# Preparing output weights behind the first exponentials, and placing one weight matrix with GpSimd

## What is computed

```python
q = rope(norm(x) @ Wq.T); k = rope(norm(x) @ Wk.T)          # bf16
o = where(causal, exp(q @ k.T / 128**0.5), 0).sum(-1)       # one number per row
a = relu(o @ fc1_w.T + fc1_b) @ fc2_w.T + fc2_b             # 1 -> 16 -> 128
x = x + norm(a)
h = relu(norm(x) @ W1[1] + b1[1])                           # the gate always picks expert 1
y = h @ W2[1] + b2[1]
x = x + norm(y)
```

## Time and profile before

| | |
|---|---|
| median of 3 runs | 93.13 us (92.77 to 93.2) |
| profiled execution | 92.96 us, its span 91.2 us |
| TensorE busy | 82.5 us, 90% of the span |
| VectorE busy | 78.5 us, 86% |
| ScalarE busy | 70.7 us, 78% |
| GpSimd busy | 59.2 us, 65% |
| granted TensorE clock | 0.992 of full speed |

### The profile page before, as it was taken

The page is one execution under the profiler, slowest core; times in us unless marked ns, Lnnn a source line. Parts: engine busy times, 40 slices in busy tenths (PEclk is TensorE's granted clock), DMA queues, the critical chain, the costliest instruction groups (busy, mean ns, idle before and its releaser), DMA issues.

```text
span 91.2 us, 1530 instructions
## 1 busy us (share of the span) xinstructions
PE 82.5 (90%) x445; PEld 49.4 (54%) x445; DVE 78.5 (86%) x205; ACT 70.7 (78%) x201; POOL 59.2 (65%) x84
## 2 busy tenths in 40 slices
PE   4958999988899789998999999999999999999930
PEld 1327465544354145433553368684575985599920
DVE  4469998999998999999998988998799689894961
ACT  5035899996998899999999999988669629545750
POOL 6497887808700697976914058587799944995590
PEclk9999999999999999999999999999999999999996
DMA  1989988830505050005000000000403101205283
GB/s 39 268 252 298 285 267 227 208 88 0 115 7 115 7 115 4 0 0 115 0 0 0 7 0 0 0 0 0 115 0 90 36 4 53 62 0 163 67 235 110
DMA packets 11884, 7.64 MB, mean 84 GB/s; under 512 B 851, under 2 KB 10980, under 8 KB 11876
## 3 DMA queue, kind: packets, MB, share of 16 engines
q1 hardware_dynamic: 11876, 7.55, 30.6%
HBM read 3.61 MB, written 2.10 MB: 63 GB/s over the span
## 4 chain that ended last, share of the span: by engine, by line
PE 59%; ACT 14%; DVE 9%; DMA 7%; issue 3%; SPq 2%; POOL 2%; POOLq 1%; DVEq 0%
PE psum L724 19%; PE psum L798 14%; ACT psum L553 11%; PE psum L750 11%; PE psum L716 6%; DMA x_s<-x 4%; PE psum L777 3%; DMA qk_swap<-qk 3%; DVE rows_n L348 2%; POOL rstd L489 2%; ACT fc L566 2%; DVE qk_r L383 2%; DVE qk_swap L383 2%; PE psum L769 1%; DVE qk L505 1%
## 5 line engine op out<-in xcount | busy, mean ns | idle before, releaser
L489 POOL TENSOR_TENSOR rstd<-ve,half_neg 128x4 f32<-128x4 f32 (+2 forms) x38 | 35.0, 930 | 23.1 <-DVE ve L354 18.7
L553 ACT ACTIVATE psum<-psum 128x1024 f32<-128x1024 f32 (+7 forms) x48 | 36.6, 763 | 1.2 <-PE psum L754 0.8
L750 PE MATMUL psum<-qk_r 128*128 128x512 bf16 (+3 forms) x80 | 19.7, 348 | 1.7 <-DVE qk_r L417 1.0
L798 PE MATMUL psum<-w_c,hid 128*128 128x128 f32 x128 | 16.0, 277 | 0.0
L798 PEld LDWEIGHTS psum<-w_c,hid 128*128 128x128 f32 x128 | 15.5, 192 | 0.8 <-issue 0.3
L724 PE MATMUL psum<-cols_n,wqk 128*128 128x512 f32 (+1 forms) x36 | 15.8, 553 | 0.0
L724 PE MATMUL psum<-cols_n,w_c 128*128 128x512 f32 (+1 forms) x36 | 15.7, 550 | 0.0
L750 PEld LDWEIGHTS psum<-qk_r 128*128 128x128 bf16 x80 | 6.7, 98 | 13.0 <-ACT psum L553 4.8
L716 PE MATMUL psum<-ident,rows_n 128*128 128x128 f32 x64 | 10.2, 277 | 0.9 <-DVE rows_n L348 0.9
L638 DVE BATCH_NORM_STATS2 stats<-psum 128x6 f32<-128x256 f32 x23 | 8.7, 419 | 1.5 <-PE psum L798 1.0
L664 DVE SCALAR_TENSOR_TENSOR x<-psum,rstd,x_s 128x128 f32<-128x128 f32 x32 | 9.1, 343 | 1.0 <-POOL rstd L489 0.9
(11 more groups left out here) (84 smaller groups left out, 129.8 us busy)
## 6 DMA issues: line engine op xcount, KB each, us to landing
x_s<-x SPq DMA_DIRECT2D x7, 256.0 KB, 4.3
qk_swap<-qk SPq DMA_DIRECT2D x14, 128.0 KB, 2.3
out<-x_s SPq DMA_DIRECT2D x7, 256.0 KB, 2.4
table<-tables SPq DMA_DIRECT2D x3, 256.0 KB, 4.2
x_s<-x SPq DMA_DIRECT2D x2, 128.0 KB, 3.6
table<-tables SPq DMA_DIRECT2D x2, 128.0 KB, 3.8
w_f<-w SPq DMA_DIRECT2D x2, 128.0 KB, 3.2
out<-x_s SPq DMA_DIRECT2D x4, 64.0 KB, 1.7
```

Source lines behind the costliest of these rows:

```text
L489: ready[k].done(eng.tensor_tensor(rstd[:, g, STAT_SLOT[k], t], ve[:, g, STAT_SLOT[k], t], half_neg[:, 0:tiles], ALU.pow), n)
L553: exps.done(eng.activation(area, area, ACT.Exp, scale=scale_qk, accum_out=sums[:, g, s, j:j + 1]), n, j, s)
L750: mm = eng.matmul(psum[:, own[0] + i, 0:width], query, qk_r[:, g0 + c, 1, 0:width], start=True, stop=c < gb)
L798: mm = eng.matmul(bank[:, j * P:(j + 1) * P], hid[:, g, h, (j0 + j) * P:(j0 + j + 1) * P], w2_c[:, h, :], start=not seeded and h == 0, sto ...
```

## The change

Four things are edited.

1. `+fc` becomes one activation over 128x128 that writes the centred, repeated matrix into a new tile `fc2_c`.
2. A new step `fcspread` on GpSimd makes fc2 from it, with two selects over 128x512: the first copies `fc2_c` to each of the four column blocks and zeroes partitions below 32j, the second, in place, zeroes those from 32(j+1) on. `fc2` matmuls wait for it. VectorE's clearing of fc2 is gone. `+hT` waits for `fcmean` instead of `+fc`.
3. `w2mean` and `w2`, which stood apart in the front, stand together behind `exp.2.0.0`.
4. `b2mean`, which stood in the front, stands behind `exp.3.3.0`.

The order is otherwise the same, word for word.

```diff
@@ STEPS @@ (the lines wrap anew; only these words move)
-... load_table.4 k.6#4 cos.3.D w2mean.0 load_b1.0 eps1.2.D q.6#0 ... swap.4 cos.4.D w2.0 q.0#3 ...
-... k.0#2 b2mean.0 rope.3.D swap.6 ...
+... load_table.4 k.6#4 cos.3.D load_b1.0 eps1.2.D q.6#0 ... swap.4 cos.4.D q.0#3 ...
+... k.0#2 rope.3.D swap.6 ...
+... norm1.5.P scores.3.0.0#12 exp.2.0.0 w2mean.0 w2.0 +k.8.D scores.3.1.0#67 exp.3.0.0 fcspread.0 rstd1.7 rot.1#5
+sum.2.D scores.3.3.0#34 swap.8 cos.8.D exp.3.1.0 hT.2#0 rot.0#1 sin.1.D cos.0.P k.2#2 exp.3.3.0 b2mean.0 sin.0.D
@@ gpsimd @@
+            def spread_fc():
+                taken["fc"].wait(eng, 0)
+                eng.affine_select(out=fc2[:, :, :], in_=fc2_c[:, :].unsqueeze(1).to_broadcast([P, TILES, P]),
+                                  compare_op=ALU.is_ge, fill=0.0, base=0, pattern=[[-BLOCK, TILES], [0, P]],
+                                  channel_multiplier=1).then_inc(s_fc, 1)
+                eng.wait_ge(s_fc, 1)
+                fc_spread.done(eng.affine_select(out=fc2[:, :, :], in_=fc2[:, :, :], compare_op=ALU.is_ge, fill=0.0,
+                                                 base=BLOCK - 1, pattern=[[BLOCK, TILES], [0, P]],
+                                                 channel_multiplier=-1), 0)
@@ take, hT @@
-                    taken["fc"].wait(eng, 0)
+                    mean_fc.wait(eng, 0)
@@ scalar, +fc @@
-                    eng.wait_ge(s_zero_fc, 1)
-                    for j in range(TILES):
-                        r = slice(BLOCK * j, BLOCK * (j + 1))
-                        ins = eng.activation(fc2[r, j, :], bank_of("fc", 0)[r, P:2 * P], ACT.Identity,
-                                             bias=means[r, 2:3])
-                    taken["fc"].done(ins, 0)
+                    taken["fc"].done(eng.activation(fc2_c[:, :], bank_of("fc", 0)[:, P:2 * P], ACT.Identity,
+                                                    bias=means[:, 2:3]), 0)
@@ vector @@
-            eng.memset(fc2[:, :, :], 0.0).then_inc(s_zero_fc, 1)
@@ tensor, fc2 @@
                     taken["hT"].wait(eng, n)
+                    fc_spread.wait(eng, 0)
```

More of the change, by code:

```diff
@@ L43 @@
 stat1.5 load_w2.0 +fc.0 rstd1.0 norm1.6.D q.3#1 load_table.2 eps1.8.D norm1.0.D tr1.6#4 +k.3.D rstd1.8 +q.3.A k.4#0
[L44 to L77, removed]
+eps1.5.D +tr1.1.A stat1.2 swap.3 +tr1.6.A norm1.8.P tr1.0#3 stat1.7 +k.4.A q.1#1 load_table.4 k.6#4 cos.3.D load_b1.0
@@ new lines @@
+eps1.2.D q.6#0 +tr1.0.D rstd1.2 +k.6.A swap.4 cos.4.D q.0#3 sin.3.D +q.6.A tr1.8#4 load_w1.0 rstd1.5 k.0#2 rope.3.D
+swap.6 +q.0.A k.1#0 +q.1.A norm1.2.D scores.2.3.0#3 +tr1.8.A scores.2.1.0#1 cos.6.D scores.2.0.0#5 exp.2.3.0
+scores.2.2.0#6 tr1.2#7 sin.4.D +k.1.A q.8#4 exp.2.1.0 cos.1.D exp.2.2.0 rope.4.D k.8#0 +k.0.A +tr1.2.A eps1.7.D +q.8.D
+norm1.5.P scores.3.0.0#12 exp.2.0.0 w2mean.0 w2.0 +k.8.D scores.3.1.0#67 exp.3.0.0 fcspread.0 rstd1.7 rot.1#5 sum.2.D
+scores.3.3.0#34 swap.8 cos.8.D exp.3.1.0 hT.2#0 rot.0#1 sin.1.D cos.0.P k.2#2 exp.3.3.0 b2mean.0 sin.0.D
@@ new lines @@
+scores.3.2.0#56 rope.1.D +k.2.A q.2#7 rope.0.D +hT.2 sin.6.D exp.3.2.0 scores.0.1.0#2 scores.0.2.0#0 tr1.5#3 sin.8.D
+w1.0#4 +q.2.A sum.3.D rope.8.D fc2.2#56 exp.0.1.0 swap.2 +tr1.5.A cos.2.D hT.3#7 scores.7.1.0#12 +w1.0.A rope.6.D
+scores.0.3.0#3 +hT.3 q.5#4 exp.7.1.0 stat3.2.D norm1.7.P k.5#7 +q.5.D exp.0.2.0 exp.0.3.0 eps3.2.D scores.5.3.0#12
+sin.2.D exp.5.3.0 +k.5.D rstd3.2 scores.8.3.1#34 rope.2.D swap.5 exp.8.3.1 x1.2 cos.5.P scores.1.3.0#12 fc2.3#07
+exp.1.3.0 stat4.2 scores.1.0.0#56 scores.0.0.0#3 tr1.7#4 stat3.3.D exp.1.0.0 scores.1.2.0#12 +tr1.7.D exp.0.0.0
@@ new lines @@
+eps3.3.P scores.1.1.0#56 exp.1.2.0 rstd3.3 sum.0.D sin.5.D q.7#4 exp.1.1.0 eps4.2.P x1.3 hT.0#1 scores.5.1.0#23
+rstd4.2 +hT.0 scores.8.2.1#56 exp.5.1.0 rope.5.D fc2.0#01 +q.7.D norm4.2.P scores.4.2.1#7 exp.8.2.1 scores.4.1.1#2
+stat3.0.D scores.4.0.1#3 k.7#4 exp.4.2.1 stat4.3 eps3.0.P scores.4.1.0#56 exp.4.0.1 rstd3.0 sum.1.D exp.4.1.1 +k.7.D
+trz.2#7 exp.4.1.0 scores.7.0.0#23 eps4.3.D +trz.2.D swap.7 rstd4.3 x1.0 exp.7.0.0 scores.5.0.0#45 norm4.3.P hT.1#6
+h1.2#7 exp.5.0.0 stat4.0 scores.8.2.0#23 eps4.0.D +h1.2.D scores.4.2.0#01 +hT.1 rstd4.0 exp.8.2.0 scores.4.3.0#45
@@ new lines @@
+cos.7.D trz.3#7 sin.7.D h0.2#6 exp.4.3.0 +trz.3.D norm4.0.P scores.4.0.0#23 +h0.2.D exp.4.2.0 scores.4.3.1#7 trz.0#4
+rope.7.D fc2.1#56 exp.4.3.1 +trz.0.D scores.6.0.0#01 exp.4.0.0 stat3.1.D h0.0#4 eps3.1.D exp.6.0.0 rstd3.1
+scores.6.3.0#23 +h0.0.D h0.3#7 exp.6.3.0 sum.4.D x1.1 hT.4#4 scores.6.2.1#01 +hT.4 scores.6.2.0#23 exp.6.2.1 stat4.1
+scores.6.0.1#45 h1.0#6 +h0.3.D exp.6.0.1 fc2.4#01 exp.6.2.0 +h1.0.D scores.6.1.0#45 eps4.1.D stat3.4.D scores.6.3.1#67
+rstd4.1 exp.6.1.0 y.2#2 eps3.4.D rstd3.4 norm4.1.D b2.0 exp.6.3.1 b2split.0 x1.4 scores.5.0.1#4 scores.5.2.1#5
@@ new lines @@
+exp.5.0.1 scores.5.1.1#3 scores.5.2.0#67 exp.5.2.1 bias.2.D scores.5.3.1#4 exp.5.1.1 scores.6.1.1#01 exp.5.2.0 trz.1#5
+stat5.2.D h1.3#3 +trz.1.D eps5.2.P exp.6.1.1 rstd5.2 stat4.4 scores.8.3.0#67 y.0#5 exp.5.3.1 b2rows.0 eps4.4.P
+exp.8.3.0 rstd4.4 sum.5.D sum.6.D +h1.3.D hT.5#4 norm4.4.P scores.7.0.1#67 ys.2 +hT.5 scores.7.1.1#01 exp.7.0.1
+bias.0.D hT.6#3 h0.1#4 out.2.P +hT.6 stat5.0.D exp.7.1.1 fc2.5#67 eps5.0.P store.2 h1.1#3 stat3.5.D sum.7.D fc2.6#01
++h0.1.D eps3.5.P +h1.1.A rstd3.5 trz.4#2 stat3.6.A hT.7#3 y.1#4 rstd5.0 x1.5 eps3.6.A +trz.4.A rstd3.6 sum.8.D +hT.7
@@ new lines @@
+ys.0 h1.4#2 stat4.5 out.0.P h0.4#5 bias.1.D eps4.5.A +h1.4.A x1.6 fc2.7#3 rstd4.5 store.0 +h0.4.A hT.8#2 y.3#6
+stat5.1.A stat4.6 norm4.5.P stat3.7.D eps3.7.A eps4.6.D +hT.8 rstd4.6 trz.5#0 bias.3.D y.4#1 +trz.5.A stat5.3.D
+rstd3.7 norm4.6.D eps5.3.A x1.7 rstd5.3 fc2.8#0 trz.6#3 stat3.8.A out.3 h0.5#2 +trz.6.A eps3.8.A stat4.7 h1.5#5
+store.3 rstd3.8 stat5.4.D eps4.7.A +h0.5.A h0.6#6 rstd4.7 eps5.1.D x1.8 +h1.5.A rstd5.1 eps5.4.D h1.6#2 stat4.8
++h0.6.D y.5#5 rstd5.4 +h1.6.A norm4.7.D eps4.8.D rstd4.8 ys.4 norm4.8.D trz.7#1 out.1 out.4.P stat5.5.A y.6#2 +trz.7.D
@@ L78 @@
+eps5.5.A store.4 rstd5.5 store.1 trz.8#1 stat5.6.D h0.7#4 +trz.8.A h1.7#6 +h0.7.A eps5.6.P h0.8#1 +h1.7.D rstd5.6
+h1.8#0 out.5 +h0.8.A y.7#6 +h1.8.A y.8#1 stat5.7.A out.6 store.5 y.10#5 eps5.7.P stat5.8.A rstd5.7 y.9#0 stat5.10.A
+eps5.8.D store.6 out.7 rstd5.8 stat5.9.A eps5.10.D store.7 rstd5.10 eps5.9.A out.8 store.8 rstd5.9 out.10 store.10
+out.9 store.9
 """
@@ L197, in build @@
         fc2 = sb("fc2", [P, TILES, P], F32)
+        fc2_c = sb("fc2_c", [P, P], F32)
         b1_s = sb("b1_s", [P, HC], F32)
@@ L229, in build @@
         s_blank, s_ident, s_center, s_mask, s_repeat = (sem(n) for n in ["blank", "ident", "center", "mask", "repeat"])
-        s_zero_fc, s_zero_b2, s_split = sem("zero_fc"), sem("zero_b2"), sem("split")
+        s_fc, s_zero_b2, s_split = sem("fc_blocks"), sem("zero_b2"), sem("split")
         def signal(name, owner):
@@ L247, in build @@
         mean_b2, b2_done = signal("b2mean", "act"), signal("b2", "act")
+        fc_spread = signal("fcspread", "pool")
         b2_split, b2_rows = signal("b2split", "pool"), signal("b2rows", "dve")
@@ L481, in _ @@
                     make_mask()
+                elif name == "fcspread":
+                    spread_fc()
                 elif name == "repeat":
```

## The result

The changed kernel's median over four executions is 94.19 us beside 93.16 for the kernel before. Some executions of every kernel here take 1.5% or more longer (96.10 us of the change and 95.25 of before), so the ratios compare the others alone, and the profiles of spread_only, memset_scratch, norm5_late, norm5_mid and norm5_act are of such long executions. The ratio is 1.0124 (95% interval 1.0087 to 1.016), which on 93.13 us is +1.15 us (+0.81 to +1.49). Forecast was +0.82, and 93.95 us. The profiled execution took 94.05 us with a span of 92.3, 1.09 more than the 92.96 of before.

The account below looks back on a forecast made before the run. TensorE bounds to 17.15 us, VectorE to 24.23, TensorE to 30.85, ScalarE to 41.33, then TensorE. Terms -0.06 - 0 - 0 + 0 + 0.88 = +0.82 us, from 93.13 to 93.95; whole range 92.5 to 94.6.

Parts of the forecast that it names:

- The stop by the selects: Near 18 us, two GpSimd selects of 0.62 us each stop VectorE's two-input products, costing 0.88 us together.
- no blocking: Rival: selects do not stop VectorE; only late w2 and b2mean preparation costs; 93.35 us, chance 0.17.
- One fc activation: In ScalarE's front, 1.10 us of work removed mostly becomes waiting for q.3; path gain 0.06 us.
- ScalarE sets the front: Rival: the 1.10 us of fc comes off at 11.8, TensorE's dense rows being only modelled ends; 92.03 us, chance 0.15.
- Clearing fc2: Early on VectorE, removing this 0.48 us gains 0, because VectorE then idles 1.63 us for the first x.
- the emptier front: Taking 1.70 us of w2mean, w2 and b2mean off ScalarE's front gains nothing; TensorE is dense up to 17.15.
- w2 behind the delay: Unit 3's first exponential slips to about 22.1 us; w2 on ScalarE ends at 21.9, so its move costs 0.
- Nothing takes it back: After VectorE hands over at 24.23 + 0.88, dense TensorE and ScalarE stages carry the delay to the end.
- The size: Whole kernel: +0.82 us, giving 93.95 us for the median.
- The price of late preparation if nothing else delays: Without blocking, ScalarE is 0.95 us late at 24; idle 0.67 absorbs most, leaving 0.28 at 30.85; chance 0.17.
- Which products: On VectorE near 18 us, cos.6 and sin.4 or their neighbours take 1.0 to 1.1 us instead of 0.68.

Follow-up runs that it names:

- spread_only: Against the kernel before: only the new fc part (one activation, two GpSimd selects), w2mean, w2 and b2mean at their old places; ratio 1.0063 (1.0018 to 1.0107).
- memset_scratch: Kernel before plus two write-only GpSimd memsets on scratch tiles at the place of fcspread; ratio 0.9965 (0.9922 to 1.0007).
- norm5_late: Kernel before with norm1.5 moved later on GpSimd, behind cos.0 near 22 us; ratio 0.9978 (0.9931 to 1.0025).
- norm5_mid: Kernel before with norm1.5 moved on GpSimd to behind rstd1.7, ahead of cos.0, near 21 us; ratio 1.0043 (1.0003 to 1.0083).
- norm5_act: Kernel before with norm1.5 on ScalarE instead of GpSimd, and w2 and b2mean behind the exponentials; ratio 1.0124 (1.0033 to 1.0216).
- select_scratch: Kernel before plus two GpSimd selects on scratch tiles nobody reads, at the place of fcspread, and a small VectorE clearing; ratio 1.012 (1.0023 to 1.0217).
- memset_again: Second profile of the kernel before plus two write-only GpSimd memsets on scratch tiles; the execution took 93.03 us.
- the second comparison: The whole change run once more against the kernel before; ratio 1.019 (1.0109 to 1.0271), profiled execution 94.16 us.
- moves_only: Kernel before with only w2mean, w2 and b2mean moved behind the exponentials, fc part unchanged; ratio 1.0027 (0.9966 to 1.0087), profiled execution 93.33 us.
- spread_early: The whole change with the selects ahead of norm1.8 on GpSimd, against the kernel before; ratio 1.0123 (1.0031 to 1.0215), profiled execution 93.2 us.

## Why the prediction was right, point by point

*The stop by the selects* (0.88 us): right in mechanism and size. Two products lengthened by 0.87 together; a select's own length 0.63 to 0.64 us, 0.62 forecast. select_scratch and memset_again separate it from the dependency and from writing. The reason given, that the nearest rows are reads on the same tiles, was not needed: the selects of select_scratch share no tile with anyone and stop as much. The rival "no blocking" falls.

*One fc activation* (gain 0.06): right. The 1.10 us became a wait of 1.08 for q.3. "+q.3" starts 1.92 us behind the start of its four matmuls, against 1.96 before: 0.04. The chain of before had named ScalarE, with TensorE's product ready only 0.06 us earlier. In the profile after, even this small gain did not reach sin.3: VectorE came to it late from cos.4, which had waited for the table. The rival "ScalarE sets the front" falls, and so does its reading of the dense rows as modelled.

*Clearing fc2* (0) and *the emptier front* (0): right. The freed time is in the waits of 0.91 us in front of "+k.6" and 0.92 in front of the first exponential.

*w2 behind the delay* (0): right. ScalarE was free 0.34 us before unit 3's first exponential.

*Nothing takes it back*: right. From VectorE's handing over it is 6.62 us to the full ScalarE stage in both, 10.48 through it in both, and 49.87 and 49.83 from its end to the end of the span.

*The size*: forecast +0.82, measured +1.15 (0.81 to 1.49). In the profile, 0.87 are the stops, and 0.26 came before sin.3, by the wait for the table, a term that the sum did not have. memset_again shows that this wait comes without the moves. Whether it is part of the ratio's excess over 0.82 stays open; the forecast lies inside the interval without it, but only just, and the second comparison (1.019, from 1.0109) is above it. What bears the 0.82 out is the 0.8 us of the table of profiles, not the ratios alone.

*The price of late preparation if nothing else delays* (0.28, the no-blocking rival): too high. moves_only was 0.56 late at the first exponential and 0 at the full stage. I had let idle time of 0.67 us take part of 0.95; in moves_only it took all that arose.

*Which products*: the text said cos.6 and sin.4 or their neighbours. The profile after has cos.6 and sin.4, the other four with selects there have norm1.2 and cos.6.

## What to carry to other kernels

Before work is moved to an idle GpSimd, look at what VectorE does at that moment: if it runs a product with two inputs in SBUF while GpSimd reads SBUF, VectorE lost in these runs the GpSimd operation's length less about 0.2 us (0.86 of 1.04, 0.44 of 0.64), and that counts in full where VectorE bounds the stage. When the chain names an engine, look for the second-latest releaser; its lead is all that speeding up the first can give. By spread_early and norm5_late, moving the colliding operation helps only if its new place has VectorE on PSUM sources or row statistics, and if what it pushes back has such a place too.
